# Weight quantization inside a gated attention and feed-forward kernel: small scale steps in another form and place, and the gate stage's scales half a round earlier

## The reference

```
x = x + tanh(g_xattn) * attention(layernorm(x), ctx)     # 16 heads of 64, causal mask
x = x + tanh(g_ffn)   * ffn(layernorm(x))                # 512 -> 1536 -> 512
```

```
def lpbq_dequant(w):                       # w_gate, w_up (1536 x 512), w_down (512 x 1536)
    wb = w.reshape(O, I // 32, 32)
    s  = max(max|wb| over the block / 7, 1e-12)
    return (clip(round(wb / s), -8, 7) * s).reshape(O, I)
x = act_qdq(x);  up = act_qdq(x @ W_up.T);  gate = act_qdq(x @ W_gate.T)
gate = act_qdq(gate * fixed_u16(sigmoid(gate)));  o = act_qdq(gate * up);  return o @ W_down.T
```

## Time and profile before

| | |
|---|---|
| time, median of 3 runs (lowest to highest) | 1419.35 us (1419.12 to 1421.72) |
| profiled execution: its own time, its span | 1418.45 us, 1416.7 us |
| PE busy | 1287.6 us, 91% |
| DVE busy | 1047.0 us, 74% |
| ACT busy | 641.2 us, 45% |
| POOL busy | 259.3 us, 18% |
| mean granted TensorE clock | 0.965 |
| first stage ends, second begins (first gate matmul) | at about 540 us |
| last job of the second stage turned | at about 817 us |

### The profile page before, as it was taken

How to read it: one execution, slowest core, us unless ns; L and a number is a source line. 1 busy time by engine, 2 the same in 40 slices (tenths; PEclk the granted TensorE clock), 3 DMA queues, 4 the chain that set the end, 5 groups by cost and what they waited for, 6 DMA issues and landing times. The chain is left out here.

```text
span 1416.7 us, 19275 instructions
## 1 busy us (share of the span) xinstructions
PE 1287.6 (91%) x6272; PEld 770.7 (54%) x6272; DVE 1047.0 (74%) x1501; ACT 641.2 (45%) x766; POOL 259.3 (18%) x311
## 2 busy tenths in 40 slices
PE   7899999999899999999999999999993039999998
PEld 6777877777787874545454444444441014444443
DVE  0488779878877666777777779999999994545554
ACT  3433343343343224444343256566677984343431
POOL 1024224224322321000000035650110000000000
PEclk9999999999999999999999999999996569999999
DMA  8002212212221345655553589994457863454543
GB/s 326 1 31 89 75 45 83 95 37 74 74 67 52 112 134 192 205 196 204 193 204 127 180 294 306 305 305 165 144 197 295 314 242 130 160 184 154 181 158 116
DMA packets 111243, 228.28 MB, mean 161 GB/s; under 512 B 23120, under 2 KB 35408, under 8 KB 111184
## 3 DMA queue, kind: packets, MB, share of 16 engines
q1 hardware_dynamic: 110896, 227.58, 46.7%
q10 hardware_dynamic: 288, 0.00, 0.0%
HBM read 136.32 MB, written 91.23 MB: 161 GB/s over the span
## 5 line engine op out<-in xcount | busy, mean ns | idle before, releaser
L1782 PE MATMUL pD<-Wh,xph 128*128 128x512 f16 x384 | 145.5, 379 | 1.0 <-DVE xpl L1757 1.0
L1268 PE MATMUL gpG<-xph,Wh 128*128 128x512 f16 x384 | 145.7, 380 | 0.0
L1268 PE MATMUL gpG<-xpl,Wh 128*128 128x512 f16 x384 | 145.5, 379 | 0.0
L1268 PE MATMUL gpG<-xph,Wl 128*128 128x512 f16 x384 | 145.5, 379 | 0.0
L1268 PE MATMUL pU<-xph,Wh 128*128 128x512 f16 x384 | 145.5, 379 | 0.0
L1268 PE MATMUL pU<-xpl,Wh 128*128 128x512 f16 x384 | 145.5, 379 | 0.0
L1268 PE MATMUL pU<-xph,Wl 128*128 128x512 f16 x384 | 145.5, 379 | 0.0
L1782 PE MATMUL pD<-Wl,xph 128*128 128x512 f16 x384 | 145.5, 379 | 0.0
L1782 PE MATMUL pD<-Wh,xpl 128*128 128x512 f16 x384 | 145.5, 379 | 0.0
L1164 ACT ACTIVATE gst<-gpG,rw 128x512 f32<-128x512 f32 x96 | 66.2, 689 | 152.9 <-PE gpG L1268 152.9
L1195 DVE TENSOR_REDUCE gmx<-gst 128x512 f32 (+1 forms) x96 | 65.6, 683 | 67.9 <-ACT gst L1164 67.9
(11 more groups left out here) (219 smaller groups left out, 2676.6 us busy)
## 6 DMA issues: line engine op xcount, KB each, us to landing
dub<-up_d SPq DMA_DIRECT2D x42, 768.0 KB, 4.7
gate_d<-gst SPq DMA_DIRECT2D x96, 256.0 KB, 2.1
gb<-gate_d SPq DMA_DIRECT2D x24, 768.0 KB, 6.5
up_d<-ust SPq DMA_DIRECT2D x72, 256.0 KB, 4.5
eu<-up_d SPq DMA_DIRECT2D x22, 768.0 KB, 6.1
xr<-xn_d SPq DMA_DIRECT2D x9, 1024.0 KB, 6.0
xin<-in_x SPq DMA_DIRECT2D x32, 256.0 KB, 2.8
x_d<-x SPq DMA_DIRECT2D x32, 256.0 KB, 2.0
```

Source lines behind the costliest of these rows:

```text
L1268: mm = pe.matmul(ps[:, :], Ws[:, it, kt * P:(kt + 1) * P], xs[:, kt, :], start=(kt == 0 and Ws is Wh and xs is xh), stop=(kt == KT - 1 and ...
L1782: mm = pe.matmul(pD[4 * t + q][:, :], os_[n][:, cs], Ws[:, it, :], start=(it == 0 and os_ is oh and Ws is Wh), stop=(it == IT - 1 and os_ ...
```

## The change

It has four parts.

1. The small tiles of the scale steps (`sn`, `rm`, `mx`, `s`) get a stride: every number takes 8 bytes, of which the first 4 are used. `inv` stays dense.
2. With one row unit, line 266 becomes a `tensor_scalar` whose second scalar is the column `t`, and line 270 a `tensor_scalar` whose scalar is the column `f`. So each has one tensor input where it had two. With three row units both stay as they are.
3. In the first stage, DVE takes `job_scale` behind `xl` and no longer ahead of it.
4. In the gate stage, `job_scales` is called once ahead of the loop for the first three jobs, then at it = 9 of the first half for jobs 3 to 5 and at it = 9 of the second half for the first three jobs of the next round, ahead of `job_integer` at the same it. The warming matmuls ahead of the stage are 4 and were 7.

```
-        self.sn = sb(ph, f"{tag}sn", [P, NJ, NBLK], F32)
+        self.sn = sb(ph, f"{tag}sn", [P, NJ, NBLK, 2], F32)[:, :, :, 0]
...                                     # rm, mx and s in the same way
-    dve.scalar_tensor_tensor(out=unit, in0=rm, scalar=-(2.0 ** 23) / ROW_TOP, in1=t, op0=ALU.mult, op1=ALU.add)...
+    if rows == 1:
+        dve.tensor_scalar(unit, rm, -(2.0 ** 23) / ROW_TOP, t, ALU.mult, ALU.add)...
+    else:
+        dve.scalar_tensor_tensor(out=unit, in0=rm, scalar=-(2.0 ** 23) / ROW_TOP, in1=t, op0=ALU.mult, op1=ALU.add)...
...
-    dve.tensor_tensor(sn, s, f.unsqueeze(2).to_broadcast(dims), ALU.mult)...
+    if rows == 1:
+        dve.tensor_scalar(sn, s, f, None, ALU.mult)...
+    else:
+        dve.tensor_tensor(sn, s, f.unsqueeze(2).to_broadcast(dims), ALU.mult)...
...
                 if have(k - 1):
                     sums(b, k - 1)
-                q = job_at(k, jobs, 0)
-                if q is not None:
-                    job_scale(dve, J, b, q, unit[:, 3 * q + b:3 * q + b + 1])
...                                     # here xl of tile k + 1
                 some(8)
+                q = job_at(k, jobs, 0)
+                if q is not None:
+                    job_scale(dve, J, b, q, unit[:, 3 * q + b:3 * q + b + 1])
...
-                        if it == 0:
-                            job_scales(dve, J, i, q, row_unit[1][...] if t == 0 else row_unit[2][...])
+                        if it == 9 and t == 0:
+                            job_scales(dve, J, i, 3, row_unit[2][:, bass.ds(i, 1)])
+                        if it == 9 and t == 1 and not last:
+                            job_scales(dve, J, i, 6, row_unit[1][:, bass.ds(3 * i + 3, 3)])
                         if it % 4 == 1:
                             job_integer(dve, J, i, q, (10 * i, 5 * t + 5))
...
+            job_scales(dve, J, 0, 0, row_unit[1][:, 0:3])
             with dve.Fori(0, FT // 2 - 1) as i:
...
-            keep_warm(pe, pG[2][:, :], ident, 7)
+            keep_warm(pe, pG[2][:, :], ident, 4)
```

More of the change, by code:

```diff
@@ L219, in __init__ @@
         self.lo = [sb(ph, f"{tag}lo{n}", [P, 512], F16) for n in range(NJ)]
-        self.sn = sb(ph, f"{tag}sn", [P, NJ, NBLK], F32)
-        self.rm = sb(ph, f"{tag}rm", [P, 3, 3], F32)
-        self.mx = sb(ph, f"{tag}mx", [P, NJ, NBLK], F32)
-        self.s = sb(ph, f"{tag}s", [P, NJ, NBLK], F32)
+        self.sn = sb(ph, f"{tag}sn", [P, NJ, NBLK, 2], F32)[:, :, :, 0]
+        self.rm = sb(ph, f"{tag}rm", [P, 3, 3, 2], F32)[:, :, :, 0]
+        self.mx = sb(ph, f"{tag}mx", [P, NJ, NBLK, 2], F32)[:, :, :, 0]
+        self.s = sb(ph, f"{tag}s", [P, NJ, NBLK, 2], F32)[:, :, :, 0]
         self.inv = sb(ph, f"{tag}inv", [P, NJ, NBLK], F32)
@@ L265, in row_units @@
     after(2)
-    dve.scalar_tensor_tensor(out=unit, in0=rm, scalar=-(2.0 ** 23) / ROW_TOP, in1=t, op0=ALU.mult, op1=ALU.add).then_inc(J.row_done, 1)
+    if rows == 1:
+        dve.tensor_scalar(unit, rm, -(2.0 ** 23) / ROW_TOP, t, ALU.mult, ALU.add).then_inc(J.row_done, 1)
+    else:
+        dve.scalar_tensor_tensor(out=unit, in0=rm, scalar=-(2.0 ** 23) / ROW_TOP, in1=t, op0=ALU.mult, op1=ALU.add).then_inc(J.row_done, 1)
     after(3)
@@ L269, in row_units @@
     after(4)
-    dve.tensor_tensor(sn, s, f.unsqueeze(2).to_broadcast(dims), ALU.mult).then_inc(J.row_done, 1)
+    if rows == 1:
+        dve.tensor_scalar(sn, s, f, None, ALU.mult).then_inc(J.row_done, 1)
+    else:
+        dve.tensor_tensor(sn, s, f.unsqueeze(2).to_broadcast(dims), ALU.mult).then_inc(J.row_done, 1)
 def job_scale(dve, J, i, q, unit):
@@ L284, in job_scales @@
 def job_scales(dve, J, i, q, unit):
-    part = slice(q, q + 3)
-    for n in range(q, q + 3):
-        dve.wait_ge(*at(J.loaded[n], 16 * i, 16))
+    c = q % J.R
+    part = slice(c, c + 3)
+    for n in range(c, c + 3):
+        dve.wait_ge(*at(J.loaded[n], 16 * i, 16 * (q // J.R + 1)))
         dve.tensor_reduce(J.mx[:, n, :], blocks(J.w[n][:, :]), X, ALU.max, apply_absolute_value=True).then_inc(J.max_done, 1)
@@ L294, in job_scales @@
     done = (10 * i, 5 * (q // 3))
-    if q < 3:
+    if c < 3:
         row_units(dve, J, done, J.s[:, part, :], J.sn[:, part, :], unit, None)
@@ L1199, in extremes @@
                         q = 3 * t + it // 4
-                        if it == 0:
-                            job_scales(dve, J, i, q, row_unit[1][:, bass.ds(3 * i, 3)] if t == 0 else row_unit[2][:, bass.ds(i, 1)])
+                        if it == 9 and t == 0:
+                            job_scales(dve, J, i, 3, row_unit[2][:, bass.ds(i, 1)])
+                        if it == 9 and t == 1 and not last:
+                            job_scales(dve, J, i, 6, row_unit[1][:, bass.ds(3 * i + 3, 3)])
                         if it % 4 == 1:
```

## The result

The changed kernel takes 1440.58 us (median of 4 runs, 1427.88 to 1443.99), 1.26% more than the kernel before: the ratio is 1.0126, with a 95% interval from 1.0102 to 1.015. The forecast was 1430 us with a range of 1410 to 1437 us. The direction was right, the size was not: the change cost about 20 us where 11 were expected, and the time lies above the range.

A forecast was written before the change was run, and what follows sets the result against it. PE, busy 91% of the span, was taken to bound the kernel. Terms -20.8 - 4.6 - 0.8 + 29.3 + 8.2 = +11.3 us on 1418.45 us gave about 1430 us, range 1410 to 1437 us.

The forecast's parts named there:

- xl ahead of the scale: First stage: PE's nine waits for xl go, -23.8 us, less 3 us for DVE falling behind, giving -20.8 us.
- The stride: Small scale tiles: 8-byte spacing was taken to change nothing, steps still waiting for POOL; rival that it frees them, 0.23.
- Gate scales at it = 9: Gate stage: scales delay the next job's integers, so PE waits seven times, +29.3 us; bounds 20.3 and 32 us.
- The sign that was named: Gate stage, it = 9: line 320 above 0.45 us would show the integers waiting for POOL.
- The old waits: Gate stage, it = 0: PE's five waits for the integers of a half's first job go, -4.6 us.
- The clock: Gate stage: half clock behind five of seven new waits, 1.65 us each, +8.2 us; rival that it stays up, 0.14.
- Start of the gate stage: Ahead of the gate loop: three fewer warming matmuls let PE start earlier, counted as -0.8 us.
- Slower: Whole kernel slower by at least 0.2%, 2.8 us: first two cases and half of the third, chance 0.72.
- all clock losses: Gate stage, upper end of the range: the clock's upper bound of 11.6 us, 3.4 us more than charged.
- the upper bound of the waits: Gate stage, upper end of the range: the seven new waits of PE at 32 us, where 29.3 us was forecast.

The follow-up runs named there:

- e9: Changed kernel with integers ahead of scales at it = 9, and first-stage block maxima and block scales moved ahead of the probabilities' sums: 1388.18 us, ratio 0.9768.
- e3: Changed kernel with 18 useless warming matmuls on PE in each of the seven gate-stage waits: 1422.85 us, ratio 1.0019.
- e8: Changed kernel with 8 useless warming matmuls, not 18, in each of the seven gate-stage waits: 1427.83 us, ratio 1.0048.
- e10: Changed kernel with integers ahead of scales at it = 9, and seven warming matmuls ahead of the gate stage, not four: 1393.63 us, ratio 0.9807.
- e7: Kernel before with only the two one-input forms for one row unit; dense tiles, scale ahead of xl, old gate stage: 1408.89 us, ratio 0.9906.
- e2: Kernel before with only the gate stage's new order (scales ahead of the loop and at it = 9, four warming matmuls): 1461.04 us, ratio 1.0286.

## Why the prediction was wrong in size

- **xl ahead of the scale, -20.8 us.** Right, 2 us too good: the nine waits went, DVE fell behind instead, and the job steps kept 4.8 us over the 153.8 us of a gapless PE, where 3 us were charged. The stage gained 18.6 us. DVE was late next, as said, though PE met it first at the residual (2.6 us in six waits) and not at the probabilities' product.
- **The stride.** Right: it frees nothing. The Trainium skill's rule in "Vector Engine (DVE) Microarchitecture Reference", section 5.1, which names no step among the conditions for the two-port mode, agrees: 0.82 us with and without the stride. What kept steps clear of POOL here was the order (line 284, 0.19 us in e9) and, for a step on one number, one tensor input in place of two (line 267, 0.21 us, where line 266 took 0.65 us).
- **Gate scales at it = 9.** Right: seven waits, 28.0 us against 29.3 predicted, 3.9 us in first halves and 4.2 in second ones. In first halves the integers do wait for POOL, but only in line 323 (1.42 us, 0.69 before). The sign that was named, line 320 above 0.45 us, did not come: it took 0.41 us. The old waits, 4.6 us, went.
- **The clock, +8.2 us, with a bound of 11.6 us.** This is the step that failed. It took the size of a fall from the first stage, 1.65 us a time, as if it were a constant, and let only the number of falls vary. Measured: seven falls of 6.8 us each, not five of 3.4. The gate stage's account is 41.3 = 28.0 - 4.6 - 0.9 (earlier start) + clock, so the clock cost 18.8 us, 2.7 us a time; part of each fall lies in the gap itself and costs nothing. e3 gives the same number from the other side: 18 us come back with the gaps filled. The price of 1.65 us was right for the short falls, which e8 puts at 1.7 us each; behind waits of 4 us they were twice as long. With 18.8 in place of 8.2 us the sum would have been 1440 us. The mechanism was right, and this term was too small.
- **Start of the gate stage, -0.8 us.** Right by luck. The first gate product came 2.06 us behind the first warming matmul, and 2.94 us in the kernel before: 0.9 us. But it comes 2.06 us behind with seven warming matmuls too (e10), which then take 1.67 us. In the trace of the kernel before they took 3.15 us because the clock was low there:

```profile
537.28:540.22 2.94, 2.94 (x8) 1.02 (x9) 2.31 (x5) 2.84 (x5) 0.00 (x0) 0.50 0.32 121
```

- **Two sums.** Slower should have had 0.45 + 0.23 + 0.07 = 0.75, not 0.72; and all clock losses with the upper bound of the waits give 1436 us, not 1437. Neither changes the outcome.

The Trainium skill, "TensorE: Matmul & The Clock Gate", in its section "HAM oscillation — how this bites in real kernels" (HAM is its name for the block that sets TensorE's clock), tells of a kernel in which every tile's wait throws the array back to the slow clock and the price is paid once a tile. The trace agrees in kind: all seven half rounds, 2.7 us each. The prediction saw that the new waits were twice as long as any in the rows, yet let only the count of the falls grow. None of its rows showed a wait of 4 us, so its upper bound should have left room for longer falls.

## What to carry to other kernels

A gap on TensorE has two prices: its own length, and the slow stretch that can follow it. None was seen behind the nine waits of 1.3 to 1.8 us in e7. Behind those of 2.0 to 2.5 us there were 3.4 us of half clock in some cases and none in others, and not by length (e8). Behind those of 4 us there were 6.8 us in all seven cases of the changed kernel, and in five of seven in e2, with 3.4 us in the other two. Filling the gaps with useless matmuls gave back 18 us (e3) though the work came no earlier. When work is moved ahead "half a round early", place it behind whatever the bounding engine waits for next: two calls in the other order were worth 47 us here. And a small VectorE instruction that waits for GpSimd can be moved to where GpSimd is idle: 0.82 us became 0.19 us (e9).

## What the runs showed of the hardware that I had not expected

- The half-rate stretches behind the waits looked at came in two lengths, 3.4 and 6.8 us. A wait of 4.06 us was followed by either (e2), and one of 2.16 us by none at 234.31 us in the kernel before, where one of 2.05 us at 249.41 us was followed by 3.4 us. The changed kernel's gate stage keeps a strict beat: the late turns of rounds 0 to 3 start at 558.79, 600.04, 640.85, 682.03, 722.80 and so on, 41.0 us apart on the mean, with a fall at each. One of its four runs took 1427.88 us at a mean clock of 0.968, the others 1440 to 1444 us at 0.954 to 0.956. What decides between them stays open; no run tried it.
- A tensor_scalar with a column in place of its second constant takes 0.21 us for one number (line 267), not the 0.15 us of line 264.
- Where three divisions of POOL follow each other, a waiting VectorE instruction (line 274) ended at 556.95 us, just behind the second of them (556.91 us); the third then took 1.32 us in place of 1.05, and the three 3.33 us in place of 3.06. The waiting instruction seems to get in between two of POOL's.
